# A four-layer metaformer with routed experts: the last image's routing cut into small parts, row additions moved between engines

## The reference

```python
logits = x @ gate_w + gate_b                      # 8 or 16 experts
top_w, top_i = top_k(logits, K)                   # K = 1 in layer 0, 2 in layers 1, 2, 3
y = sum over chosen e of  w_e * (act(x @ W1[e] + b1[e]) @ W2[e] + b2[e])
t = t + y
```

## Time and profile before

| what | value |
|---|---|
| median of 3 | 2166.95 us |
| the profiled execution | 2167.17 us, of it 2165.3 us span |
| TensorE busy | 1759.8 us (81%) |
| DVE busy | 1550.8 us (72%) |
| ACT busy | 1202.5 us (56%) |
| POOL busy | 965.0 us (45%) |
| mean granted TensorE clock | 0.899 |

### The profile page before, as it was taken

How to read it: one execution, slowest core, us unless ns; L and a number is a source line. 1 busy time by engine, 2 the same in 40 slices (tenths; PEclk the granted TensorE clock), 3 DMA queues, 4 the chain that set the end, 5 groups by cost and what they waited for, 6 DMA issues and landing times. The chain is left out here.

```text
span 2165.3 us, 44723 instructions
## 1 busy us (share of the span) xinstructions
PE 1759.8 (81%) x10964; PEld 1390.0 (64%) x10981; DVE 1550.8 (72%) x4800; ACT 1202.5 (56%) x2719; POOL 965.0 (45%) x965
## 2 busy tenths in 40 slices
PE   2687666897498878899996776787859999979996
PEld 2233666897443434699995433777747777778996
DVE  8898887679677777755887676646866677755575
ACT  5455776796532323577786333555755444446664
POOL 0000234446104435475753277776630354457765
PEclk8799667998699999999998788689979999989998
DMA  3002002232120011132531112235422011113365
GB/s 81 0 0 78 17 26 62 60 88 81 22 76 30 30 52 36 44 95 80 162 98 54 53 51 79 69 94 157 147 75 98 21 37 32 53 53 105 102 199 154
DMA packets 183594, 154.30 MB, mean 71 GB/s; under 512 B 40294, under 2 KB 162822, under 8 KB 183362
## 3 DMA queue, kind: packets, MB, share of 16 engines
q1 hardware_dynamic: 153410, 92.37, 15.7%
q0 software_dynamic: 29952, 59.26, 8.1%
HBM read 85.33 MB, written 68.79 MB: 71 GB/s over the span
## 5 line engine op out<-in xcount | busy, mean ns | idle before, releaser
L1759 POOL DMA_INDIRECT returned<-rows_second_choice x488 | 491.4, 1007 | 302.3 <-DVE rows_second_choice L1680 102.6
L1310 POOL DMA_INDIRECT dispatched<-rows_first_choice,slot x192 | 190.4, 992 | 492.2 <-DVE rows_second_choice L1206 440.0
L1539 PE MATMUL psum<-rows_first_choice 128*128 128x128 f32 x2816 | 386.7, 282 | 19.2 <-DVE rows_first_choice L1661 19.0
L1539 PEld LDWEIGHTS psum<-rows_first_choice 128*128 128x128 f32 x2816 | 353.5, 197 | 24.2 <-DVE rows_first_choice L1661 23.0
L1549 PE MATMUL psum<-expert_weights,rows_first_choice 128*128 x2240 | 324.7, 284 | 24.1 <-DVE rows_second_choice L1677 13.0
L1549 PEld LDWEIGHTS psum<-expert_weights,rows_first_choice 128*128 128x128 f32 x2240 | 284.8, 196 | 34.2 <-issue 30.0
L1609 ACT ACTIVATE rows_first_choice<-psum,bias_columns 128x128 f32<-128x128 f32 x832 | 238.7, 373 | 96.6 <-PE psum L1539 95.0
L1310 POOL DMA_INDIRECT dispatched<-rows_second_choice,slot x192 | 187.1, 975 | 58.5 <-issue 58.2
L1310 POOL DMA_INDIRECT dispatched<-rows_first_choice,expert_weights x64 | 61.9, 967 | 266.3 <-DVE rows_first_choice L1204 248.9
L1592 ACT ACTIVATE rows_first_choice<-expert_weights 128x512 f32 x216 | 136.9, 634 | 45.5 <-issue 44.3
L1531 PE MATMUL psum<-identity,rows_second_choice 128*128 128x128 f32 x488 | 137.9, 284 | 6.3 <-DMA rows_second_choice<-dispatched 6.1
(11 more groups left out here) (424 smaller groups left out, 3840.0 us busy)
## 6 DMA issues: line engine op xcount, KB each, us to landing
rows_second_choice<-dispatched SPq DMA_DIRECT2D x488, 65.0 KB
rows_second_choice<-returned SPq DMA_DIRECT2D x10, 1024.0 KB, 5.3
returned<-rows_second_choice POOLq DMA_INDIRECT x488
expert_weights<-in_L_ffn_w SPq DMA_DIRECT2D x3, 2048.0 KB, 8.3
expert_weights<-returned SPq DMA_DIRECT2D x6, 1024.0 KB
channel_major<-returned SPq DMA_DIRECT2D x6, 1024.0 KB, 6.0
residual<-in_x SPq DMA_DIRECT2D x8, 512.0 KB, 8.0
rows_second_choice<-returned SPq DMA_DIRECT2D x8, 512.0 KB, 3.9
```

The costliest lines, as they stand in the source:

```text
L1310: pool.indirect_dma_start(out=self.k.dispatched, out_offset=bass.IndirectOffsetOnAxis(ap=self.slot[:, b % 2, c, t:t + 1], axis=0), in_=sel ...
L1539: ins = pe.matmul(k.ps[:, self.PSH + u % 2, j * P:(j + 1) * P], self.wc[:, u % 2, j * P:(j + 1) * P], self.xt[:, u % 2, :], start=True, st ...
L1759: pool.indirect_dma_start(out=k.returned[0:N * self.K, :], out_offset=bass.IndirectOffsetOnAxis(ap=self.rt[:, u, C:C + 1].bitcast(I32), ax ...
```

## The change

Five things are done.

1. The routing of image 7 is cut into parts: add and statistics, norm in quarters (on ACT) or halves (on DVE), choose in four, place in four, plan in three. They are spread over 17 steps in layer 0 and 22 in layers 1 to 3. The sends of image 7 start at step 11, 17, 17 and 18 instead of 8, 9, 12 and 16, with the same spacing.
2. On DVE the part of a step now stands behind the gate, the scaling and the guard, on ACT behind the activation.
3. `tiles` writes out two groups of 16 tiles instead of one where there are more than one (layers 1 to 3).
4. After layer 0 the row additions go from POOL to DVE, each as two halves, with new steps `add` and `collect`.
5. `STEPS` after layers 1 and 2 are moved: turns three steps apart instead of two, and after layer 2 the additions stand at steps 90 to 123 instead of 78 to 125, closer together.

The core of the diff (the split methods hold the same operations as before and are left out, but for the places where the cuts are):

```diff
 class NormStage:
...
-        dict(load=(55, 56, 60, 64, 68, 71), fold=(43, 44, 48, 52, 56, 60), collect=(50, 52, 54, 58, 63, 67),
-             finish=(60, 69), root=(61, 70), offset=(62, 71), norm=(63, 65, 67, 69, 72, 74),
-             turn=(65, 67, 69, 71, 74, 76), keep=(66, 68, 70, 72, 75, 77)),
+        dict(load=(55, 56, 60, 64, 68, 71), add=(46, 48, 52, 56, 60, 66), collect=(48, 50, 54, 58, 64, 68),
+             finish=(60, 70), root=(61, 71), offset=(62, 72), norm=(63, 65, 67, 69, 73, 75),
+             turn=(65, 67, 69, 71, 75, 77), keep=(66, 68, 70, 72, 76, 78)),
...
-        dict(load=(87, 88, 89, 93, 103, 119), fold=(75, 77, 79, 83, 91, 107), add=(80, 84, 88, 92, 105, 112),
+        dict(load=(87, 88, 89, 93, 103, 119), fold=(75, 77, 79, 83, 91, 108), add=(80, 84, 88, 92, 105, 113),
...
-             turn=(105, 107, 109, 111, 125, 127),
+             turn=(105, 108, 111, 114, 126, 129),
...
-        dict(load=(87, 88, 89, 97, 103, 119), add=(78, 84, 90, 96, 116, 122), collect=(82, 88, 94, 100, 120, 126),
-             finish=(102, 128), root=(103, 129), offset=(107, 133), norm=(108, 110, 112, 114, 134, 136),
-             turn=(111, 113, 115, 117, 137, 139), keep=(112, 114, 116, 118, 138, 140)),
+        dict(load=(87, 88, 89, 97, 103, 119), add=(90, 93, 96, 99, 107, 120), collect=(94, 97, 100, 103, 111, 124),
+             finish=(105, 126), root=(106, 127), offset=(110, 131), norm=(110, 112, 114, 116, 132, 134),
+             turn=(113, 116, 119, 122, 135, 138), keep=(114, 117, 120, 123, 136, 139)),
...
-        self.adds = (None, 1, 2, 4)[layer]
+        self.folds, self.adds = layer == 2, (None, 2, 2, 4)[layer]
...
     def gpsimd_step(self, pool, t):
-            if self.adds < 4 and t == self.steps["fold"][b]:
+            if self.folds and t == self.steps["fold"][b]:
                 pool.wait_ge(self.s_back[b].h, self.s_back[b].base + 16)
-                if self.choices == 1:
-                    pool.tensor_tensor(xs, xs, room, ALU.add).then_inc(self.s["rows_added"].h, 1)
...
     def vector_step(self, dve, t):
-                for c in range(2):
-                    if self.adds == 4 and t == at["add"][b] + 2 * c + h:
+                for c in range(self.choices):
+                    if not self.folds and t == at["add"][b] + 2 * c + h:
                         self.add_half(dve, b, c, h)
...
 TAILS = [
-    dict(pe=(0, 4, 5, 7), dve=(0, 2, 6, 8, 9), act=(2, 4, 7), send={7: (8, 1)}),
-    dict(pe=(0, 4, 5, 8), dve=(0, 2, 6, 9, 10), act=(2, 4, 7), send={7: (9, 2)}),
-    dict(pe=(0, 6, 8, 12), dve=(0, 3, 9, 13, 14), act=(3, 6, 10), send={7: (12, 1)}),
-    dict(pe=(0, 6, 8, 12), dve=(0, 3, 9, 13, 14), act=(3, 6, 10), send={6: (0, 2), 7: (16, 4)}),
+    dict(add=0, finish=1, root=1, invert=2, address=6, normalise=(3, 4, 4, 5), turn=6, keep=6, copy=7, gate=8, choose=(9, 9, 10, 10),
+         rank=11, exp=11, place=(12, 12, 13, 13), plan=(14, 15, 16), send={7: (11, 1)}),
+    dict(add=0, finish=1, root=1, invert=2, address=7, normalise=(3, 4, 5, 6), turn=7, keep=7, copy=8, gate=9, choose=(10, 11, 12, 13),
+         rank=14, exp=14, place=(15, 16, 17, 18), plan=(19, 20, 21), send={7: (17, 2)}),
+    dict(add=0, finish=1, root=1, invert=2, address=7, normalise=(3, 4, 5, 6), turn=7, keep=7, copy=8, gate=9, choose=(10, 11, 12, 13),
+         rank=14, exp=14, place=(15, 16, 17, 18), plan=(19, 20, 21), send={7: (17, 1)}),
+    dict(add=0, finish=1, root=1, invert=2, address=7, normalise=(3, 4, 5, 6), turn=7, keep=7, copy=8, gate=9, choose=(10, 11, 12, 13),
+         rank=14, exp=14, place=(15, 16, 17, 18), plan=(19, 20, 21), send={6: (0, 2), 7: (18, 4)}),
 ]
...
     def tiles(self, eng, step):
-        for u in range(RING):
-            step(u, u, False)
-        looped = self.table_end // RING
-        if looped > 1:
-            with eng.Fori(1, looped) as g:
+        looped, lead = self.table_end // RING, min(2, self.table_end // RING)
+        for t in range(lead * RING):
+            step(t, t % RING, False)
+        if looped > lead:
+            with eng.Fori(lead, looped) as g:
...
             if not last and not self.vector_copies:
                 copy_weights(t + 1, (u + 1) % RING)
-            if at == root:
+            activate(t, u)
+            if at == tail["root"]:
                 route.root(act, B - 1)
...
             if not last:
                 copy_rows(t + 1, (u + 1) % RING)
-            if at == add:
-                route.add(dve, B - 1)
...
             if self.gated:
                 gate(t, u)
             if past(t, 2):
                 scale(t - 2, (u - 2) % RING)
                 if self.guard and u % 2:
                     guard(t - 3, (u - 3) % RING)
+            if at == tail["add"]:
+                route.add_rows(dve, B - 1)
...
+            if at == tail["choose"][0]:
+                route.choose_best(dve, B - 1)
...
+            if at == tail["plan"][2]:
+                route.plan_columns(dve)
```

More of the change, by code:

```diff
@@ L505, in add_late @@
         for c in range(self.choices):
-            if self.adds == 4:
+            if not self.folds:
                 self.add_half(dve, b, c, 0)
@@ L1552, in result @@
             ins.then_inc(self.s["y_ready"].h, 1)
-        back, rows, gate, rank = self.tail["pe"]
+        tail = self.tail
         def step(t, u, last):
@@ L1699, in guard @@
             assert ch.n == 6
-        add, norm, choose, place, plan = self.tail["dve"]
+        tail = self.tail
         def step(t, u, last):
@@ L1708, in step @@
                 copy_rows(t + 1, (u + 1) % RING)
-            if at == add:
-                route.add(dve, B - 1)
-            if at == norm:
-                (route.invert if route.scalar_norm else route.norm)(dve, B - 1)
-            if at == choose:
-                route.choose(dve, B - 1)
-            if at == place:
-                route.place(dve, B - 1)
-            if at == plan:
-                route.plan_second(dve)
             if self.gated:
@@ L1724, in step @@
                     guard(t - 3, (u - 3) % RING)
+            if at == tail["add"]:
+                route.add_rows(dve, B - 1)
+            if at == tail["finish"]:
+                route.add_finish(dve, B - 1)
+            if route.scalar_norm:
+                if at == tail["invert"]:
+                    route.invert_root(dve, B - 1)
+            else:
+                for h in range(2):
+                    if at == tail["normalise"][2 * h]:
+                        route.norm_half(dve, B - 1, h)
+            if at == tail["address"]:
+                route.address(dve, B - 1)
+            if at == tail["choose"][0]:
+                route.choose_best(dve, B - 1)
+            if at == tail["choose"][1]:
+                route.choose_mark(dve, B - 1)
+            if at == tail["choose"][2] and route.K == 2:
+                route.choose_next(dve, B - 1)
+            if at == tail["choose"][3]:
+                route.choose_weigh(dve, B - 1)
+            if at == tail["place"][0]:
+                route.place_ranks(dve, B - 1)
+            for c in range(route.K):
+                if at == tail["place"][1 + c]:
+                    route.place_slots(dve, B - 1, c)
+            if at == tail["place"][3]:
+                route.place_weights(dve, B - 1)
+            if at == tail["plan"][0]:
+                route.plan_levels(dve)
+            if at == tail["plan"][1]:
+                route.plan_jumps(dve)
+            if at == tail["plan"][2]:
+                route.plan_columns(dve)
             if at >= self.table_end:
```

197 lines of the change are left out of this document (120 added, 77 removed).

## The result

The changed kernel takes 2171.93 us in the median of 20 executions, the kernel before 2166.94 in the median of 20 beside them: ratio 1.0024, interval 1.0017 to 1.0031. That is slower by 5 us where 27 us faster were forecast.

The account below looks back on a forecast made before the run. Stage heads were taken as bound by a chain through DVE, ACT and TensorE, not an engine. Terms −4 − 7 − 1 − 8 − 7.5 = −27.5 us gave 2139.5 us from the median; range 2122 to 2159.

Parts of the forecast that it names:

- item 1: Layer 0, head: cut-up routing closes part of TensorE's idle time and the first send starts earlier; −4 us, bounds −10 to +3.
- item 2: Layer 0, end: row additions moved from POOL to DVE end DVE's waiting and stretching; −7 us, net gain 3.2 to 12.0.
- The rule by which this term would have come out at +1: Layer 0, end: shared VectorE and GpSimd port starves POOL's descriptors, each addition delaying a transfer; +1 at worst, set aside.
- item 3: Layer 1: head regains perhaps 4 us, the first POOL addition's stand moves there and costs 3; −1, bounds −6 to +5.
- the ring holds 16: Layer 1: results back up behind POOL's first addition, but 16 fit; given beside taking 3 us from 0 to 6.9.
- item 4: Layer 2, head: POOL sets the pace, so only its idle time can be won; −2 us, from −3 to +5.
- item 5: Layer 2, step 78: addition moved to step 90 finds its transfer landed, 10.8 less 5 us; −6, from −11 to 0.
- item 6: Layer 3, head: two thirds of TensorE's 11.8 us idle come back and are kept; −7.5 us, bounds −11.8 to +3.
- rival D: Heads of layers 0 and 3: with the holes gone the clock holds, 10 us more gained, 2129; chance 0.09.
- item 7: Two groups unrolled: only more code, no operation more or less; 0 us.
- C: All heads: parts behind the scaling make the next rows' copies late; slower by +11 us, 2178; chance 0.11.
- B: Heads: later sends and results stuck in POOL's and SP's queues eat the gain, about −15 us remain, 2152; chance 0.17.

Follow-up runs that it names:

- experiment 5: Changed kernel with all parts at their new steps but ahead of gate, scaling, guard and ACT's activation: 0.998 of the kernel before, median 2163.13 us.
- Experiment 11: Changed kernel, all parts ahead, layer 0 at tighter steps (0 to 13, sends from 9), old steps after layer 2, early small POOL addition: 0.9913 of the kernel before.
- Experiments 3: Changed kernel with the old steps of the norm after layer 2 (first addition at step 78 again): 1.0011 of the kernel before.
- 8: Changed kernel with the three 1 MB transfers after layer 2 issued at steps 87, 90, 93 instead of 87, 88, 89: 1.0017 of the kernel before, median 2170.40 us.
- 12: Changed kernel, all parts ahead, tighter layer 0 steps, early small POOL addition, additions after layer 2 at steps 86, 90, 94, 98: 0.992 of the kernel before.
- experiment 7: Kernel before with only two groups of 16 tiles written out: 1.0013 of the kernel before.

## Why the prediction was wrong

By stage, from the first tile to the last, the forecast was −11, −1, −8 and −7.5, the trace has −4.6, +6.8, +1.4 and −4.2. That is 26.9 us of the 32 between forecast and measurement; the rest is the 5 us that this trace does not hold.

1. **Layer 0, head (item 1: −4, measured +5.7).** The step that failed is "place at step 13 ends at about 361 + 13 x 1.9 + 6 + 6 = 398, and the first send, behind it, starts some 5 us earlier". The choice's first operation came at 396.05, place ended at 409.86, and the first send started 5.6 us later. And the send had not been bound by place before: it stood behind eight results, and now behind eleven, and DVE waits longer for the results that it is to scale (13.5 us in the head, 9.7 with the parts ahead, 9.2 before). With the parts ahead (experiment 5) tile 24 is 2.95 us late, which is my +3 for the later sends, right in size; the other 2.8 are the place behind the scaling. Experiment 11 shows the limit under it, which I had in the earlier trace rows: tile 24 follows POOL's first send.
2. **Layer 0, end (item 2: −7, measured −11.0; undone, 11.9).** Mechanism right, near its upper bound of 12. The rule by which this term would have come out at +1 was read too widely. In the Trainium skill, "SBUF — State Buffer", section "SBUF: two separate sides", a VectorE operation with two SBUF inputs, as these additions are, locks the shared ports only against a GpSimd operation that reads SBUF; whether POOL's transfers do that no run here shows. My row for it was one of many, too, and the half additions there stand between copies and scalings, not back to back: beside them POOL's transfers took 1.03 us in the mean and up to 1.29 (0.99 and up to 1.28 without an addition, 1490 to 1560). At the end of layer 0 the 15 that overlap an addition took 1.13 us in the mean, the longest 1.53, the 19 others 0.98. That is 2 us of POOL's time, and POOL idled 45 us of 82.
3. **Layer 1 (item 3: −1, measured +6.8).** The first POOL addition cost 5.8 (undone 7.3, warmed 5.2), not 3. The step that failed is "the ring holds 16": DVE's addition stands in the queue ahead of the tiles' copies and waited 5.65 us itself. The head lost 3.4 instead of winning 4; the place within the step is more than all of it (4.3 at tile 36, experiment 5).
4. **Layer 2, head (item 4: −2, measured −4.6).** Right in sign, too small. That POOL's pace limits it fits experiment 5: its tile 24 comes 3.1 us earlier than in the changed kernel (45.60, 48.70), its tile 78 does not (127.67, 127.06).
5. **Layer 2, step 78 (item 5: −6, measured +6.0).** This is the term that was wrong by most. "Finds the transfer landed" is true, and DVE had no wait. Counted from tile 78, the changed kernel is 12.3 us ahead at tile 87, about the 10.78 and more. The step that failed is that I counted DVE's work only and put the transfers at nothing. The three 1 MB transfers start at the same steps as before; once nobody stands, the tiles' own rows are in flight with them, which costs 9.3 us over four tiles. Then DVE's additions, with SP's stand behind them, cost 7.5 us by tile 104, where I had 5, and 1.5 more are lost by the last tile. Experiments 3, 8 and 12 keep both prices.
6. **Layer 3 (item 6: −7.5, measured −4.2 at the last tile).** The step that failed is that two thirds of TensorE's idle time come back: 1.1 of 11.8 us did. The head won 5.4, and 4.3 of these came from the clock, which I had only in rival D. Even the 12.6 us that experiment 5 wins at tile 24 end as 3.7 at the last tile, so "each us gained early is kept" was wrong, too; what takes it back no experiment separates.
7. **Two groups (item 7: 0).** The heads of layers 1 and 3 bear it out (experiment 7); the 0.13% of that run stay open.

Of the rivals, C had the sign and the cause, the place behind the scaling, and the smaller part of the mechanism. It expected the next rows' copies to be late; to tile 24 those waits grew in layers 2 and 3 alone, from 2.3 to 3.9 us and from 0.4 to 2.5, and with the parts ahead they are 1.2 and 0.4. What is late besides is the routing's own chain, from DVE to TensorE's ranks and from ACT to its transposes, and with it the clock: the wait before the rank product grew from 0.4 to 1.6 us in layer 1 and from nothing to 2.3 and 2.2 in layers 2 and 3. I gave it 0.11 for want of asking where DVE's idle time lies: ahead of the scaling, where a part is free, and not behind it. B's late sends were real in layer 0. D came in part: in layer 3's head the clock rose to 0.97 although most of the holes stayed, and that is the larger share of what the head won.

## What to carry to other kernels

Put side work of an in-order engine ahead of the instruction that waits, where its idle time is, and count each part's place within its step before its step number. Before a wait is removed, look for what else runs in its shadow: a burst of transfers that was free under it will be paid for by whoever runs instead. And when a first use is deleted, find the next one.

## What was not expected of the hardware

The stand before POOL's first addition, 6.94, 7.72, 7.47 and 7.15 us, is about the same for 128x1024 and 128x2 numbers and moves with the first addition. In all four kernels that is also the first one after POOL's maximum over the partitions, and no run parts the two.

In layer 1 a stretch of 2.57 us, of which TensorE worked 0.39 (waits of 1.64 and 0.54 us), was followed by matmuls at 0.50 of the clock. The head of before has a single wait of 1.97 us at 917.07 and shows 1.00 throughout. What parts the two cases these rows do not tell.
